# Hosting the preparation of a scan layer in the attention layer before it

## What is computed

```python
# layer 0: attention with 16 heads of 16 channels, causal; q, k, v and output projections
# layer 1 (layer 4 has the same form): a selective scan over the context
xc    = causal_conv4(in_proj_w @ ctx)              # 256 channels
u     = silu(xc + conv_b)
dt_lo, B, C = split(x_proj_w @ u)                  # 8, 16 and 16 rows
delta = softplus(dt_proj_w @ dt_lo + dt_proj_b)
state = state * exp(delta * A) + (delta * u) * B   # 16 states, over time
y     = (sum_n(state * C) + D * u) * silu(z)       # z = x, the output of layer 0's layer norm
```

## Time and profile before

| | us |
|---|---|
| median of three runs | 2292.72 (2288.64 to 2293.07) |
| profiled execution, own time | 2281.8 |
| its span | 2280.0 |
| TensorE busy | 1803.2 (79%) |
| VectorE busy | 1402.0 (61%) |
| ScalarE busy | 826.6 (36%) |
| GpSimd busy | 326.3 (14%) |

### The profile page before, as it was taken

The page is one execution under the profiler, slowest core; times in us unless marked ns, Lnnn a source line. Parts: engine busy times, 40 slices in busy tenths (PEclk is TensorE's granted clock), DMA queues, the critical chain, the costliest instruction groups (busy, mean ns, idle before and its releaser), DMA issues.

```text
span 2280.0 us, 31711 instructions
## 1 busy us (share of the span) xinstructions
PE 1803.2 (79%) x12349; PEld 1307.7 (57%) x12358; DVE 1402.0 (61%) x2504; ACT 826.6 (36%) x1929; POOL 326.3 (14%) x313
## 2 busy tenths in 40 slices
PE   7656778756726676678999979997999979999795
PEld 4523544423423345546777748886888867777552
DVE  5269956769989491545556639995555634555314
ACT  1455502145513105456666621111444424344100
POOL 2304510004510204212122100000000000000100
PEclk9975568655557798989999989998999989999766
DMA  4010020010010102040000020001002030000000
GB/s 120 7 37 1 0 63 3 2 57 1 1 47 0 27 16 76 1 129 1 1 1 1 1 79 1 1 1 47 10 10 66 1 93 1 1 1 1 38 1 19
DMA packets 29087, 55.11 MB, mean 24 GB/s; under 512 B 6742, under 2 KB 22131, under 8 KB 27388
## 3 DMA queue, kind: packets, MB, share of 16 engines
q1 hardware_dynamic: 28940, 53.10, 7.9%
HBM read 45.35 MB, written 1.05 MB: 20 GB/s over the span
## 4 chain that ended last, share of the span: by engine, by line
PE 58%; DVE 26%; issue 6%; ACT 4%; POOL 2%; DMA 2%; SPq 1%; DVEq 0%; POOLq 0%; ACTq 0%
PE banks L1770 8%; PE banks L1753 7%; PE banks L1788 6%; DVE big L968 6%; PE banks L1682 5%; DVE big L584 3%; PE banks L2519 3%; PE banks L2130 3%; PE banks L2532 3%; PE banks L485 2%; PE banks L2555 2%; PE banks L496 2%; DVE big L2224 2%; PE banks L1710 1%; DVE ln_stats L195 1%
## 5 line engine op out<-in xcount | busy, mean ns | idle before, releaser
L1863 DVE TENSOR_REDUCE arena<-banks 128x2 f32<-128x512 f32 x192 | 132.3, 689 | 351.8 <-PE banks L1753 351.8
L1991 ACT ACTIVATE big<-banks,arena 128x256 f32<-128x256 f32 x384 | 189.9, 502 | 119.2 <-DVE arena L1863 99.1
L1753 PE MATMUL banks<-big 128*128 128x256 f32 x768 | 206.8, 393 | 2.9 <-ACT big L1991 2.9
L220 POOL TENSOR_TENSOR ln_rstd<-ln_var_eps,neg_half 128x2 f32<-128x2 f32 x48 | 36.6, 763 | 1164.1 <-DVE ln_var_eps L200 1164.1
L1770 PE MATMUL banks<-big 32*128 32x256 f32 x3072 | 183.3, 386 | 11.2 <-DVE big L1881 10.0
L1788 PE MATMUL banks<-big 128*128 128x256 f32 x768 | 181.2, 381 | 0.3 <-ACT x_feat L244 0.3
L1682 PE MATMUL banks<-x_feat,arena 128*128 128x256 f32 x768 | 177.0, 384 | 0.0
L1770 PEld LDWEIGHTS banks<-big 32*128 32x128 f32 x3072 | 157.9, 188 | 31.1 <-DVE big L1881 12.4
L1753 PEld LDWEIGHTS banks<-big 128*128 128x128 f32 x768 | 137.5, 191 | 45.9 <-issue 32.5
L1682 PEld LDWEIGHTS banks<-x_feat,arena 128*128 128x128 f32 x768 | 148.7, 194 | 22.1 <-issue 1.3
L1788 PEld LDWEIGHTS banks<-big 128*128 128x128 f32 x768 | 144.7, 190 | 28.9 <-issue 9.4
(11 more groups left out here) (336 smaller groups left out, 3122.5 us busy)
## 6 DMA issues: line engine op xcount, KB each, us to landing
big<-big SPq DMA_DIRECT2D x128, 32.0 KB, 1.9
big<-in_ctx_tok SPq DMA_DIRECT2D x8, 512.0 KB, 7.7
big<-big SPq DMA_DIRECT2D x32, 64.0 KB, 2.3
arena<-in_L0f_w SPq DMA_DIRECT2D x1, 2048.0 KB, 8.2
arena<-in_L1a_wo SPq DMA_DIRECT2D x1, 2048.0 KB
arena<-in_L1f_gv SPq DMA_DIRECT2D x1, 2048.0 KB
arena<-in_L2a_qk_w SPq DMA_DIRECT2D x1, 2048.0 KB
arena<-in_L2x_q_w SPq DMA_DIRECT2D x1, 2048.0 KB
```

Source lines behind the costliest of these rows:

```text
L1753: last = mm(ps[:, h * SEQ:(h + 1) * SEQ], self.q[:, n % 2, r, h * P:(h + 1) * P], k, start=not self.mask, stop=True, skip_group_check=self ...
L1863: ins = v.tensor_reduce(dst, B[4 + u % 2][:].rearrange("p (h k) -> p h k", h=2), AX.X, ALU.max, negate=True)
L1991: last = a(self.probs[:, u % 3, h, :], B[4 + u % 2][:, h * SEQ:(h + 1) * SEQ], ACT.Exp, bias=self.neg_max[:, u % 4, h:h + 1], scale=scale, ...
```

## The change

It adds the notion of a guest: layer 0 gets a reference to layer 1's block (`host`) and calls pieces of its preparation at places between its own units. Layer 1 then begins with the first spread.

- SyncE loads `ctx_feat`, the guest's projection weights and `small` first of all, before `x_feat` (before, the context came after layer 0's moves, and the guest's weights at the end of layer 0's queue); the guest's other weights come before layer 0's moves.
- TensorE: the context projection is its first work, in banks 0 to 3; low and dt stand between the two phases, in banks 4 to 7. dt now has a bank for each quarter, so TensorE doesn't wait for ScalarE between them. `score_t` of unit 1, which uses these banks, waits for the guest's last Abs.
- ScalarE: evictions first; Silus behind layer 0's evictions; low's eviction (on VectorE before), Relu and Abs between the phases; Exp and squares behind the exponentials of the units.
- VectorE: convolution before layer 0's V; in the units, behind each copy, a piece of the split of B and C (12 pieces, units 0 to 11), `pick` in unit 12, and the products; `delta` and `delta * u` behind layer 0's normalisation.
- Squares, products, `delta` and `delta * u` are in quarters (128x512) now, 16 + 16 + 4 + 4 instructions in place of 4 + 4 + 1 + 1. This and the new order of the pieces hold for layer 4 too, which has no host.
- `room` of the guest is layer 0's tile `stage`, free once Q and K are moved.
- The branches of the older way are gone.

```diff
+        if self.guest:
+            self.guest.tensor_in(pe)
         e.wait_x_feat(pe, l)
         for blk in range(2):
             pe.wait_ge(self.prepared, blk + 1)
+            if blk and self.guest:
+                pe.wait_ge(self.guest.s_padded, 4)
...
         turn_max(G - 1)
+        if self.guest:
+            self.guest.tensor_low(pe)
+            pe.wait_ge(self.max_read, G)
+            self.guest.tensor_dt(pe)
...
+            if u == 1 and self.guest:
+                pe.wait_ge(self.guest.s_dt_act, 4)
...
                                   e.banks[:, slot:slot + 2, 3 * P:4 * P]).then_inc(self.sum_read, 1)
+            if self.guest:
+                self.guest.vector_beside(dve, u)
...
+        if self.guest:
+            self.guest.vector_delta(dve)
...
         read_max(G - 1)
+        if self.guest:
+            self.guest.scalar_low(act)
+            self.guest.scalar_dt(act)
         for u in range(self.units):
...
+            if self.guest:
+                self.guest.scalar_beside(act, u)
...
+    def squares_at(self, u):
+        return () if u < 2 else (2 * u - 4, 2 * u - 3) if u < 4 else (u,)
+
+    def vector_beside(self, dve, u):
+        if u < 2 * self.PARTS:
+            self.vector_parts(dve, u)
+        elif u == 2 * self.PARTS:
+            self.vector_pick(dve)
+        for k in self.squares_at(u):
+            self.vector_factor(dve, k)
+
+    def scalar_beside(self, act, u):
+        for q in ((2 * u, 2 * u + 1) if u < 2 else ()):
+            self.scalar_tiny(act, q)
+        for k in self.squares_at(u):
+            self.scalar_square(act, k)
...
-            1: lambda l: StateSpace(e, l, e.arenas[l % 2], "L0x"),
+            1: lambda l: StateSpace(e, l, e.arenas[l % 2], "L0x", room=blocks[0][1].room()),
...
+            if which == 1:
+                blocks[0][1].host(blocks[-2][1])
...
         def _(sp):
+            sp.dma_start(e.ctx_feat[:], dram["ctx_feat"]).then_inc(e.ctx_loaded, 16)
+            blocks[0][1].guest.load_in(sp)
             sp.dma_start(e.x_feat[:], dram["x_feat"]).then_inc(e.x_feat_loaded, 16)
```

More of the change, by code:

```diff
@@ L349, in sync @@
             sp.dma_start(dst, src).then_inc(self.w_loaded, 16)
-        if self.hosts:
-            self.beside.load(sp)
+        if self.guest:
+            self.guest.load(sp)
         e.wait_x_feat(sp, l)
@@ L374, in sync, with host @@
                 sp.dma_start(self.q[row:row + 1, g, :], self.max_rows[8 * j:8 * j + 8, g, :]).then_inc(self.rows_moved, 16)
-    def host(self, beside):
-        self.beside = beside
+    def host(self, guest):
+        self.guest = guest
     def room(self):
         return self.stage.rearrange("p s k t -> p (s k t)")
[L383 to L392, removed]
     def slot(self, u):
@@ L504, in tensor @@
                 score_t(u + self.slots - 1)
-            for n in self.second_slots(u):
-                self.beside.tensor_slot(pe, n)
             sum_up(u)
@@ L594, in vector @@
             slot = self.slot(u)
-            for n in self.second_slots(u):
-                self.beside.vector_slot(dve, n)
             dve.wait_ge(self.summed, u + 1)
@@ L769, in __init__ @@
             big.reset()
+        self.in_bank = 0 if self.hosted else 4
         self.u = big.take(CH, TOKENS)
@@ new lines, in quarter, with vector_factor @@
+    def quarter(self, tile, q):
+        j, half = divmod(q, 2)
+        return tile[:, j, half * BANK:(half + 1) * BANK]
+    def vector_factor(self, dve, k):
+        i, q = divmod(k, self.QUARTERS)
+        of = lambda tile: self.quarter(tile, q)
+        dve.wait_ge(self.s_squared, k + 1)
+        if i:
+            dve.wait_ge(self.s_factor, k - self.QUARTERS + 1)
+        self.e.nc.vector.scalar_tensor_tensor(of(self.delta), of(self.square[i % 2]), FACTORS[i][1], of(self.delta if i else self.tiny),
+                                              ALU.add, ALU.mult).then_inc(self.s_factor, 1)
@@ L1088, in gpsimd @@
     def gpsimd(self, pool):
-        if not self.hosted:
-            self.wait_start(pool)
-            self.gpsimd_clear(pool)
-            for s in range(STEPS):
-                self.gpsimd_slot(pool, s)
+        self.wait_start(pool)
+        self.gpsimd_clear(pool)
+        for s in range(STEPS):
+            self.gpsimd_slot(pool, s)
 DH = 128
```

275 lines of the change are left out of this document (123 added, 152 removed).

## The result

| | before | after |
|---|---|---|
| median of four runs, us | 2291.68 (2288.64 to 2293.07) | 2254.20 (2252.83 to 2255.56) |
| ratio, with 95% interval | | 0.9841 (0.9808 to 0.9874) |
| profiled execution, own time | 2281.8 | 2253.0 |
| mean granted clock in it | 0.845 | 0.847 |

A forecast was written before the change was run, and what follows sets the result against it. VectorE and TensorE share the load, neither full; layer 1's start was a chain of engines waiting in turn. Terms -46.7 + 0.2 + 6.1 + 2.5 + 4.9 + 1.1 - 1.9 = -33.8 from 2292.7 gave 2258.9 us, range 2247 to 2270.

The forecast's parts named there:

- 1, layer 1: Layer 1's start: first scan 4.7 us after the last turned tile, at 133.9 instead of 180.6, -46.7 us.
- 2, start: Start of layer 0: qk_w lands later, but the new matmuls take over TensorE's slow passes; net +0.2 us, at worst +1.8.
- 3, between the phases: Layer 0 between the phases: low, dt, Relu, Abs and table load put the first exponential at 74.9, +6.1 us.
- 4 and 5, the units: Layer 0's 16 second-phase units: engine time alone +2.5 us, VectorE and GpSimd waiting for each other +4.9.
- 6, after the units: Behind layer 0's last normalisation: eight VectorE operations delay the layer norm, +1.1 us, or +1.7 at 0.69 each.
- 7, layer 4: Layer 4, the unhosted second scan with the same code: products start earlier, -1.9 us, or 0 at 0.69 a piece.
- the upper bound: Layer 0's units: the second mask waits for one whole VectorE piece in every unit, 9.9 us.
- what would show it: Signs of a right forecast in layer 0: units from the fourth on 2.4 to 2.9, masks above 0.63 in the mean.
- rival (b): Layer 0's units: every unit blocked fully, +5.0 us more, perhaps +4 for products; 2264 to 2268, chance 0.15.
- (c): TensorE's clock falls in layer 0's lengthened units and in low: +7 us for six units, 2266, chance 0.10.
- (d): Slower than before: masks, pieces and exponentials serialise in layer 0's 16 units, 6.4 us each; 2316, chance 0.02.
- (e): Layer 1's preparation is not gone: its new first step waits for more than the turned tiles; 2290, chance 0.01.

The follow-up runs named there:

- the repeat of before: The kernel before, run again unchanged and profiled a second time: median 2291.69 us over ten runs, profile span 2286.4.
- experiment 2: Four kernels, each one edit to the changed kernel: pick between the phases 2251.38 us, pick and split there 2250.44, Exp table early 2256.17, Relu on VectorE 2257.65.
- the early table: Changed kernel with -exp(A) moved right behind the Silus, so the Exp table is loaded before the units: 2256.17 us, ratio to before 0.9850.

## Why the prediction was right

Forecast 2258.9, measured 2254.2: in the range of 2247 to 2270, and faster. That the two lie so near is in part luck. Profile against profile the working gave -33.8 (2248.0) and the trace has -28.8 (2253.0), 5.0 less; the medians lie 37.5 apart, because the profiled execution of before was 9.9 below its median and that of the changed kernel only 1.2. By its own steps, profile against profile:

| step | predicted | measured |
|---|---|---|
| 1, layer 1 | -46.7 | -46.6 (4.75 from last tile to first scan) |
| 2, start | +0.2 | +1.7 |
| 3, between the phases | +6.1 | +4.8 |
| 4 and 5, the units | +7.4 | +7.4 |
| 6, after the units | +1.1 | +0.9 (4.74 against 3.86), and +1.1 for slower turns and layer norm |
| 7, layer 4 | -1.9 | -1.2 |
| layer 6, not forecast | 0 | +4.3 |

The rows add up to -27.6, and the last eviction of layer 11 moved by 27.8.

**Steps 1, 6 and 7** hold. In 7 the first scan came 2.0 earlier, 0.1 from the forecast; behind it the sums of the same layer took 0.9 more at a lower clock.

**Step 2** was mis-sized. The matmuls for the context did take over the slow passes (they ran from 5.14 to 10.27, and the 32 passes of Q and K then took 13.97 instead of 15.44), but the first use of qk_w came 3.1 later, not 1.8, and this decided: layer 0's first maximum is taken 1.74 later. The step gave the issues ahead of it 0.2; qk_w was issued 1.41 later (2.66 against 1.25), and from there to its first use it was 8.64 instead of 6.95. Yet 1.7 is a difference of two executions: the first maximum stands at 32.76, 34.17 and 34.81 in the three profiles with before's code up to there, and between 33.80 and 35.52 in the eleven with the change's. Against the repeat of before the step is +0.3.

**Step 3** forecast 74.9 with the clock at the lower level and named +4.5 for full clock. The exponential came at 75.32 with a start 1.74 later, so +4.8: low ran at full clock (3.63 for the eight passes). In other profiles it did not: from the last turn to the first exponential it is 6.16 before and 10.95 in the shown profile after, but 12.5 to 12.7 in four kernels whose edits lie elsewhere, which is +6.4 to +6.5. So the lower level in low, as the step had it, was the more frequent case (seven of ten profiles), and the shown profile is the other. The chain of copy, dt, eight evictions and table load was right piece by piece.

**Steps 4 and 5** are right in the sum and wrong in the parts; that the sums agree is luck. Eleven ordinary units grew by 1.27 in all (11 x 0.115), where half of the upper bound had been taken, 4.9. What filled the sum was the pick, 3.9 instead of 1.0, some 1.7 of it the clock that fell during its wait (experiment 2), and the first interval, at the lower level, with 1.4 over 2.39; the rest, 0.6, lies between the first exponential and the first copy. The contention is there and mutual, as the earlier trace rows had it. The masks' mean went from 634 to 765 ns, so the condition named under what would show it (above 0.63) is met, though as a sign it was weak: 634 already meets it. But in a pair it costs the masks at most 0.34 and most of that is taken up before TensorE sums. The Trainium skill (SBUF — State Buffer, Who interferes with whom) says of the engine that did not issue first that it "fully blocks". The pick agrees, where three masks took 4.31 instead of 2.0 beside a cast of 2.48, and so do the ends of masks and pieces, 0.50 and 0.54 behind each other. In the ordinary units such a block lasts only as long as what is left of the other's instruction, and full blocking in every unit, rival (b), didn't occur.

**The rivals.** (c) came true in small: the clock did fall in the units, at two places; one interval of 3.8 stands at the start and one behind the pick. Neither (d) nor (e) has a row for it; the longest interval is 4.95, one of fifteen.

**The 3.7 us that were over.** The profile's sum gives 28.8 and the medians 37.5. The forecast took the shown execution's offset to the median of three, 10.9, and carried it over to the changed kernel as a constant. It isn't one. The profiled execution of before was one in which all sixteen units ran at the upper level. In the repeat five intervals did not, and against that profile layers 0 and 1 together are 42.3 us shorter after, not 30.8. The change fills TensorE's idle time from 62.9 to 67.06 with low and dt. With it there were one to three such intervals at the start of the units in the five profiles in which that start is as the change has it, so a part of the gain may be that before meets the lower level for longer. That is argued, not shown: there are two profiles of before, the changed kernel's 145.10 for the end of layer 0 is itself the shortest of its three (147.77 and 148.36), and the kernels with the early table and with Relu on VectorE had six. What decides between one and six was not settled.

## What to carry to other kernels

Read how long a stage takes in more than one execution before a single trace is made the scale: the second phase of layer 0 ran at either clock level in executions of one kernel, and its time then differed by 7.5 us, more than most of the terms that were being added up. A hosted piece costs what it meets: short pieces on VectorE beside GpSimd's masks cost a tenth of a microsecond per unit, one long one (2.3 us) cost 3.9, a fall of the clock included, and 3.3 of that came back once it stood where VectorE was idle anyway. Fillers and earlier starts are to be judged over the whole kernel: two of them won in their stage and lost it in another.

## What was not expected of the hardware

- Identical kernels, 33 us apart: 2272.29 to 2305.12 in nineteen runs of before, at mean clocks of 0.852 and 0.836.
- Layers whose code no kernel touches take one of two times: layer 3 74.5 or 69.1, layer 7 357.5 or about 361.9. Layer 6, untouched by the change, went from 218.9 to 223.2 and stayed there in the repeat. When layer 6 gained 7.5 us by a steadier clock, layer 7 took 4.2 more.
- A VectorE instruction on 128x2 took 2.29 us (before 1.37) at the start of layer 0. GpSimd clears 128x4096 from 12.72 to 16.37, and this instruction ends at 16.40; before, the clearing ended at 13.25 and it at 13.27. It was over when GpSimd was:

```profile
14.11 2.29 DVE L534 TENSOR_SCALAR arena<-arena 128x2 f32<-128x2 f32 x1 [1.19 <-DMA arena<-in_L0a_qk_b]
```

```profile
12.72 3.65 POOL L667 MEMSET big<- 128x4096 f32 x1
```
